# First head's operands copied within SBUF, and the last node of a two-branch attention block made with features on partitions and direct products

## The reference

```python
x  = attn_x                          # (2, 1024, 128)
xn = layernorm(x)
out = x + attn(xn) + ffn(xn)

def attn(x):     # 16 heads of 8, causal, rotary embedding on q and k
    q, k, v = split_heads(x @ qkv_w.T + qkv_b)
    p = softmax(where(causal, rope(q) @ rope(k).T / sqrt(8), min))
    return merge_heads(p @ v) @ out_w.T + out_b

def ffn(inputs): # 6 nodes; each an unmasked attention with 8 heads of 16
    nodes = {-1: inputs}
    for c in range(6):
        q = ew[c,0] * (nodes[c-1] @ We[eq] + be[eq])
        k = ew[c,1] * (nodes[in_k] @ We[ek] + be[ek])
        v = ew[c,2] * (nodes[in_v] @ We[ev] + be[ev])
        nodes[c] = act_w[c] * mha(q, k, v, Wq[c], Wk[c], Wv[c], Wo[c]) + q
    return layernorm(nodes[5]) * ln_g + ln_b
```

## Time and profile before

| what | value |
|---|---|
| median of three timed runs | 1428.02 us (1425.81 to 1428.82) |
| profiled execution, its own time | 1432.52 us |
| its span, first to last instruction | 1430.7 us |
| mean granted clock of TensorE | 0.986 of 2.4 GHz |
| PE busy | 1388.9 us (97%) |
| DVE busy | 1256.0 us (88%) |
| ACT busy | 1137.6 us (80%) |
| POOL busy | 447.0 us (31%) |

### The profile page before, as it was taken

How to read it: one execution, slowest core, us unless ns; L and a number is a source line. 1 busy time by engine, 2 the same in 40 slices (tenths; PEclk the granted TensorE clock), 3 DMA queues, 4 the chain that set the end, 5 groups by cost and what they waited for, 6 DMA issues and landing times.

```text
span 1430.7 us, 60748 instructions
## 1 busy us (share of the span) xinstructions
PE 1388.9 (97%) x26482; PEld 931.6 (65%) x26482; DVE 1256.0 (88%) x1557; ACT 1137.6 (80%) x2127; POOL 447.0 (31%) x932
## 2 busy tenths in 40 slices
PE   6899999999999999999999999999999999999996
PEld 5467777656667566676676665766667666667662
DVE  8788999898989889899898898998989989989784
ACT  3378888688878878888788788887888878878793
POOL 5331114334322332233323332234223432330110
PEclk9899999999999999999999999999999999999997
DMA  8131112344232332333323223333233332321212
GB/s 251 36 126 50 59 51 95 118 130 140 71 122 83 122 106 69 100 105 101 107 80 125 99 76 100 106 114 107 75 100 106 97 109 78 127 97 56 64 40 64
DMA packets 115940, 138.22 MB, mean 97 GB/s; under 512 B 14954, under 2 KB 90347, under 8 KB 115547
## 3 DMA queue, kind: packets, MB, share of 16 engines
q1 hardware_dynamic: 115675, 134.33, 29.0%
HBM read 64.90 MB, written 62.26 MB: 89 GB/s over the span
## 4 chain that ended last, share of the span: by engine, by line
PE 84%; DMA 5%; SPq 4%; DVE 3%; ACT 2%; POOL 2%; issue 1%; ACTq 0%; POOLq 0%; DVEq 0%
PE s L992 51%; PE cps L1087 24%; PE misc L992 8%; DMA qs<-mrows 3%; SPq L419 1%; ACT probs L761 1%; DMA dram_raw_b<-csb 1%; DVE neg_max L942 1%; PE misc L987 1%; SPq L387 1%; SPq L456 1%; DMA ks<-dram_qk_a 0%; DMA ks<-dram_qk_b 0%; POOL parts L585 0%; POOL xtok L644 0%
## 5 line engine op out<-in xcount | busy, mean ns | idle before, releaser
L761 ACT ACTIVATE probs<-s 128x512 f32<-128x512 f32 x1792 | 1059.2, 599 | 227.7 <-PE s L992 166.0
L942 DVE TENSOR_REDUCE neg_max<-s 128x1 f32<-128x1024 f32 x768 | 936.2, 1222 | 71.2 <-PE s L992 16.4
L992 PE MATMUL s<-qs,ks 99*32 99x512 bf16 (+2 forms) x7680 | 808.4, 371 | 8.6 <-DMA qs<-mrows 6.7
L992 PE MATMUL s<-ks,qs 96*32 96x512 bf16 (+2 forms) x7680 | 606.7, 370 | 6.3 <-DMA ks<-dram_qk_a 4.1
L1087 PE MATMUL cps<-probs,vs 128*32 128x256 f32 (+1 forms) x7552 | 590.8, 368 | 0.3 <-ACT probs L761 0.3
L992 PEld LDWEIGHTS s<-qs,ks 99*32 99x32 bf16 x7680 | 235.6, 94 | 245.2 <-ACT probs L761 101.4
L1087 PEld LDWEIGHTS cps<-probs,vs 128*32 128x32 f32 x7552 | 314.4, 110 | 77.5 <-issue 17.1
L992 PEld LDWEIGHTS s<-ks,qs 96*32 96x32 bf16 x7680 | 290.4, 97 | 90.5 <-issue 24.7
L617 POOL TENSOR_TENSOR mparts<-neg_max,zeros 128x8 bf16<-128x8 f32 x128 | 25.8, 201 | 788.7 <-DVE neg_max L942 657.1
L938 DVE CUSTOM_DVE_ANT_0 s<-s,mask_q 128x1024 f32<-128x1024 f32 (+7 forms) x256 | 188.2, 786 | 27.5 <-PE s L992 17.8
L683 POOL TENSOR_TENSOR parts<-full,zeros 128x512 bf16<-128x512 f32 x48 | 61.5, 1282 | 52.8 <-DVE full L918 52.8
(11 more groups left out here) (128 smaller groups left out, 603.2 us busy)
## 6 DMA issues: line engine op xcount, KB each, us to landing
dram_qk_b<-parts SPq DMA_DIRECT2D x48, 384.0 KB, 3.3
qs<-dram_qk_b SPq DMA_DIRECT2D x96, 192.0 KB
ks<-dram_qk_b SPq DMA_DIRECT2D x96, 192.0 KB
dram_qk_b<-parts SPq DMA_DIRECT2D x48, 256.0 KB, 3.2
dram_raw_b<-csb SPq DMA_DIRECT2D x95, 128.0 KB, 4.4
dram_qk_b<-parts SPq DMA_DIRECT2D x48, 128.0 KB, 3.2
vsrc<-srcT SPq DMA_DIRECT2D x12, 512.0 KB, 3.2
ctx_b<-dram_raw_b SPq DMA_DIRECT2D x44, 128.0 KB
```

Of the source, the lines that this page charges most:

```text
L761: nc.scalar.activation(buf[:, lo:hi], s2[bank][:, 0:hi - lo], ACT.Exp, scale=scale).then_inc(exp_done, 1)
L942: last = ve.tensor_reduce(peak, scores, AX.X, ALU.max, negate=True)
L992: last = te.matmul(dst[c0:c0 + STRIP, :], lhsT[:, c0:c0 + STRIP], rhs, start=start, stop=stop, tile_position=(0, c0))
```

## The change

Ahead of the loop:
- The layer norm of the second batch (8 tiles) moves from VectorE to GpSimd, its transposes and copies into A0 (`tr` 2 and 3). GpSimd sets the rows of ones in `ks` earlier.
- The products of the sixth node (`prod` 5) and all of the edge biases (`b0` 0 to 2, 18 matmuls of one column) move into A0; the other biases get later turns. VectorE instead of GpSimd makes the low parts n = 2, 3. `row_n` is gone.
- Head 0's second chunk is no longer read back from DRAM. Twelve copies take 8 rows of a part within SBUF from `parts` to `qs[0]` and `ks[0]`; the first chunk is written and read as before, by two loads of half the width. The writes of the second chunk follow.
- GpSimd's addition of the bias row to `xtok` moves from step 0 to step 6 of A0. Head 8 is loaded ahead of the max row of step 7, and the wait for the second batch's writes moves to the end of the first AL.

At the end:
- The last node of the first batch is made like the others (`lnode`), VectorE adds its bias, and four transposes for each chunk turn it (`fin`).
- In T only five heads of the second batch are normed through DRAM, and their sums and contexts are asked for at the end of BE. For each of the last three heads TensorE multiplies `csb` directly by that head's rows of `Wo` with a column that picks the sum (`late_head`); VectorE multiplies by the reciprocal and adds up in `fin`. The rows are placed in `late_wo` (in `ctx_a`) by twelve DMAs in BE. `TAIL_AT` puts two of these products, the skip products, the context products and the transposes of the rest into T's turns; the third product comes last.

The diff, cut to its core:

```diff
+FIN_AT = {(4, 4): ("lnode", 0), (4, 6): ("lnode", 1), (5, 1): ("fin", 0), (5, 5): ("fin", 1)}
+TAIL_AT = {(0, 2): ("direct", 0), (0, 4): ("skip", 0), (0, 6): ("skip", 1), (1, 2): ("direct", 1),
+           (1, 4): ("contexts", 0), (1, 5): ("contexts", 1), (1, 6): ("turned", 0), (1, 7): ("turned", 1)}
-START_AT = {(0, 0): ("bias", 1), (0, 1): ("bias", 2), (0, 2): ("bias", 3),
-            (0, 4): ("rot", 8), (1, 2): ("rot", 9), (1, 4): ("rot", 10), (2, 2): ("rot", 11),
+START_AT = {(0, 0): ("b0", 0), (0, 1): ("b0", 1), (0, 2): ("b0", 2), (0, 3): ("tr", 2),
+            (0, 4): ("rot", 8), (1, 0): ("tr", 3), (1, 1): ("prod", 5), (1, 3): ("bias", 1), (2, 0): ("bias", 2), (2, 3): ("bias", 3), (1, 2): ("rot", 9), (1, 4): ("rot", 10), (2, 2): ("rot", 11),
...
+            def first_head(n, part):
+
+                w, op = n // 2, n % 2
+                lo, hi, step = (Q_ROWS, K_ROWS)[op][part]
+                sp.wait_ge((rope_hi, rope_mid, a_low)[part], n + 1)
+                for r in range(lo, hi, step):
+                    sp.dma_start((qs, ks)[op][0][r * DA:(r + 1) * DA, w * CH:(w + 1) * CH], parts[n][0:DA, part, :]
+                                 ).then_inc(first_in, 16)
+
+            for n in range(NCH):
                 write_a(n, [0])
                 if n:
                     write_a(n - 1, [2])
                 write_a(n, [1])
-            write_a(2 * NCH - 1, [2])
+            sp.wait_ge(dve_const, 3 * RING)
+            first_head(2, 0)
+            write_a(1, [2])
+            first_head(2, 1)
+            first_head(3, 0)
+            first_head(2, 2)
+            for n in range(NCH):
+                sp.wait_ge(a_written[n], 3 * 16)
+                sp.dma_start((qs, ks)[n][0][0:6 * DA, 0:CH], qk_dram["A"][n, :, 0:DA, 0:CH]).then_inc(qk_in[0], 16)
+            first_head(3, 1)
+            first_head(3, 2)
+            for n in (2, 3):
+                write_a(n)
...
-                    if k == UP - 1 and kind not in ("A0", "BE", "T"):
+                    if (kind, r, k) == ("AL", 0, UP - 1):
+                        for s in a_written:
+                            sp.wait_ge(s, 2 * 3 * 16)
+                    if k == UP - 1 and kind not in ("BE", "T"):
                         load_unit(kind, r, UP, b)
...
+                    if kind == "BE" and UP - N_LATE <= k:
+
+                        n = k - (UP - N_LATE)
+                        sp.wait_ge(spread_zero, 1)
+                        for g in range(4):
+                            sp.dma_start(late_wo[g * VW:g * VW + DB, n, g, 0:D], last_wo[k * DB:(k + 1) * DB, :]
+                                         ).then_inc(spread_in, 16)
+                    if kind == "BE" and k == UP - 1:
+
+                        for n in range(2):
+                            sp.wait_ge(ctx_out[n], 16 * ((UP // 2) * (ph + 1) - 1 - n))
+                        sp.wait_ge(lnode_ps, NCH)
+                        read_before("T", 0, 1, [0], "sums")
+                        read_before("T", 0, 1, [0], "contexts")
...
+            for t in range(TB, TT):
+                pl.tensor_scalar(xn[:, t * D:(t + 1) * D], xtok[:, t * D:(t + 1) * D], mv[:, 2 * t:2 * t + 1],
+                                 rstd[:, t:t + 1], ALU.subtract, ALU.mult).then_inc(xn_late, 1)
...
-                    if kind == "A0" and k == 0:
+                    if kind == "A0" and k == 6:
 
                         pool.wait_ge(bias_used, 4)
...
+            def late_head(n, t0, tiles):
+
+                for t in range(t0, t0 + tiles):
+                    at = t % 3 * WO
+                    if t % 3 == 0 or t == t0:
+                        some = min(3 - t % 3, t0 + tiles - t)
+                        after(ve.reciprocal(rec_h[:, t:t + some],
+                                            late[t // 3][:, at + D:at + D + (some - 1) * WO + 1:WO]))
+                    dst = fin[:, S + t * D:S + (t + 1) * D]
+                    if n == 0:
+                        last = ve.tensor_scalar(dst, late[t // 3][:, at:at + D], rec_h[:, t:t + 1], None, ALU.mult)
+                    else:
+                        last = ve.scalar_tensor_tensor(dst, late[t // 3][:, at:at + D], rec_h[:, t:t + 1], dst,
+                                                       ALU.mult, ALU.add)
+                return last
...
             for n in range(1, len(FINISH)):
+                after(late_head(N_LATE - 1, FINISH[n][0] - TB, FINISH[n][1]))
                 last_moments(n)
...
+                elif what == "lnode":
+                    pe.wait_ge(ctx_ready, NORMS.after(kind, r))
+                    mm_strips(misc[:, :], last_wo, ctx_b[:, cols], stop=False)
+                    mm_strips(misc[:, :], last_we, srcT[:, (NODES - 1) * T + w * CH:(NODES - 1) * T + (w + 1) * CH],
+                              start=False).then_inc(lnode_ps, 1)
                 else:
-                    pe.wait_ge(ctx_ready, NORMS.after(kind, r))
-                    last_node(0, w, misc, ("skip", "context"))
+                    pe.wait_ge(lnode_sb, w + 1)
+                    turned(misc, full[w]).then_inc(fin_ps, 1)
...
+            def late_head(n):
+
+                pe.wait_ge(ctx_sb, UP * PHASES.before("T", 0) - N_LATE + n + 1)
+                pe.wait_ge(spread_in, 16 * 4 * N_LATE)
+                pe.wait_ge(spread_zero, 1 + N_LATE)
+                pe.wait_ge(max_done, MAXIMA.before("T", 0))
+                need(pe, dir_used, n)
+                for t in range(TB):
+                    at = t % 3 * WO
+                    last = mm(late[t // 3][:, at:at + WO], csb[(UP - N_LATE + n) % 2][:, t % 2 * 128:(t % 2 + 1) * 128],
+                              late_wo[:, n, t // 2, :])
+                last.then_inc(dir_ps, 1)
```

More of the change, by code:

```diff
@@ L439, in normed @@
                 which, heads, width = ("A", HA, DA) if kind == "B0" else ("B", HB, DB)
-                return which, heads, heads - (kind == "T"), width
+                return which, heads, heads - N_LATE * (kind == "T"), width
             def read_before(kind, r, b, which_of, what):
@@ L786, in _ @@
             walk(phase)
-            for w in range(NCH):
-                act.wait_ge(fin_ps, NCH + w + 1)
-                nc.scalar.copy(fin[:, S + w * CH:S + (w + 1) * CH], (misc, s2[0])[w][:, :]).then_inc(fin_sb, 1)
         @block.vector
@@ L944, in phase @@
-                        if NORMS.per[kind] and (k, i) == ((2, 7) if kind in ("BL", "BE", "T") else (SPREAD_AT[kind], 0)):
+                        if i == 0:
+                            need(dve, max_parts, 4 * (u - 1))
+                        n = steps_before(kind, k, 0) + i
+                        dve.wait_ge(s1_ready, MAXIMA.before(kind, r) + n + 1)
+                        for t, lo, hi in query_tiles(kind[0], i):
+                            scores, peak = s1[n % 2][:, lo:hi], neg_max[k % 2][:, t:t + 1]
+                            if kind[0] == "A":
+                                last = ve.tensor_tensor_reduce(
+                                    out=scores, in0=scores, in1=mask_q[:, S - hi + lo:S], scale=-1.0,
+                                    scalar=-MASKED, op0=ALU.add, op1=ALU.min, accum_out=peak)
+                            else:
+                                last = ve.tensor_reduce(peak, scores, AX.X, ALU.max, negate=True)
@@ L996, in _, with transposes @@
             pe.wait_ge(pool_const, 4)
-            def transposes(batch):
-                for t in range(batch * TB, (batch + 1) * TB):
-                    pe.wait_ge(xn_ready, t + 1)
-                    last = te.transpose(half[t // 4][:, t % 4 * 128:(t % 4 + 1) * 128], xn[:, t * D:(t + 1) * D],
-                                        ident[:, :])
-                    if t % 4 == 3:
-                        last.then_inc(xt_ps, 1)
+            def transposes(g, bank):
+                for t in range(4 * g, 4 * g + 4):
+                    if t < TB:
+                        pe.wait_ge(xn_ready, t + 1)
+                    else:
+                        pe.wait_ge(xn_late, t - TB + 1)
+                    last = te.transpose(bank[:, t % 4 * 128:(t % 4 + 1) * 128], xn[:, t * D:(t + 1) * D], ident[:, :])
+                last.then_inc(xt_ps, 1)
             def rotate(m, bank):
@@ L1067, in _ @@
             pe.wait_ge(rot_done, 4 * NCH)
-            biases(0)
-            for n in range(2, NODES):
-                products(n)
-            pe.wait_ge(comp_sb, 3 * NODES)
+            pe.wait_ge(comp_sb, 3 * 2)
+            pe.wait_ge(va_sb, TB // 4)
             pe.wait_ge(pool_const, N_CONST)
@@ L1142, in extra @@
                     biases(w)
+                elif what == "b0":
+                    edge_biases(w)
+                elif what == "tr":
+                    transposes(w, misc)
+                elif what == "prod":
+                    products(w)
                 elif what == "rot":
@@ new lines, in tail @@
+            def tail(what, w):
+                cols = slice(w * CH, (w + 1) * CH)
+                src = (NODES - 1) * T + S + w * CH
```

(24 more changed lines are left out.)

248 lines of the change are left out of this document (132 added, 116 removed).

## The result

The kernel after takes 1433.77 us (median of five runs, 1432.7 to 1436.13), the kernel before 1428.02 (1425.81 to 1430.58) beside it: ratio 1.0043, 95% interval 1.003 to 1.0057. It is slower by 6.1 us (4.3 to 8.1); 1426.5 was forecast, and the time lies 2.3 us above the range of 1419.5 to 1431.5. The profiled execution took 1436.13 us with a span of 1434.3.

What follows compares the result with a forecast made beforehand. TensorE, 84% of the last-ending chain, was taken as the main bound, with SP's issues at the start; +2.95 -3.3 -3.0 +7.3 -5.5 = -1.55 us took 1428.0 to 1426.5, range 1419.5 to 1431.5.

Steps and rivals of the forecast that it cites:

- Item 2: Phase A0: work moved between the first scores lengthens the first three head steps from 27.95 to 34.4 us, +6.45 us.
- rival B: Steps 0 to 2: shared-bank hand-overs cost 0.7 us each, clock falls again in step 1; 1433 us, chance 0.15.
- Item 1: Start: earlier ropes and copies inside SBUF bring the first score from 38.8 to 35.3, -3.5 us.
- Item 3: Ninth head: loading head 8 before the max row removes TensorE's gap and the clock's fall, -3.3 us.
- Item 4: Last node, first batch: products with features on partitions are cheaper, less the added transposes, -3.0 us.
- Items 5 and 6: T: inserted products and transposes are exposed, +7.3 us; after the last context 16.7 us against 22.2, -5.5 us.
- rival D: T: gathering TensorE's idle shares hides the inserted lumps by half, +3.6 instead of +7.3; 1423 us, chance 0.08.
- A: Step 0: TensorE keeps or soon regains full clock; -7.2 us with cheap issues, about 1421; chance 0.27 including issues alone.
- E: T: transposes let the clock fall, the last two direct products cost 1.4 us more each; 1429 us, chance 0.05.

Runs made afterwards that it cites:

- start_only: Start of the kernel after, with head 8's request and the tail of the kernel before: ratio 1.0046 to the kernel before, +6.6 us.
- path_only: Kernel before with head 0's second chunk copied inside SBUF, its first loaded apart, no work moved past the first score: ratio 0.9962, -5.4 us.
- after_gap: Kernel after with the edge biases and the sixth node's products issued ahead of the first score: ratio 0.9992 to the kernel before, 7.3 us below after.
- tail_only: Kernel after with the start and head 8's loads of the kernel before, only the new tail kept: ratio 0.9994 to before, -0.9 us.
- after_no_direct: Kernel after with 7 of 8 products left out of two direct groups, output incomplete: ratio 1.0016 to before, 3.9 us below after.
- after_sliced: Kernel after with the last phase's direct, skip and context products and transposes issued in slices of a few instructions: ratio 1.0042 to before.
- path_b0: path_only plus edge biases between the first scores, other biases later, POOL's input addition in step 6: ratio 1.004 to before, 5.7 us above it.
- after_filler: Kernel after with six unused 512-column matmuls in the idle stretch before the first score: ratio 1.0033 to before, 1.4 us below after.
- before_again: The unchanged kernel before, run once more for a second trace: ratio 1.0007 to the kernel before.
- gap_filler: after_gap with five unused 512-column matmuls behind the edge biases: ratio 1.0004 to the kernel before, 1.7 us above after_gap.

## Why the prediction was wrong, by its own steps

*Item 2 is the step that failed:* "what is moved into phase A0" was given +6.45 us and measured 11.7 in the trace of after (39.7 us from the first score to head 3's maxima, against 27.95) and 11.3 by start_only less path_only. A group was taken at 2.3 us and is 2.72, 1.3 us for three, and with it step 0 came to 15.7 and not 14.2 (its own terms add to 14.35 already). Step 1 was taken "at full clock again" with 9.7; the clock was at 1.2 GHz until 55.1 and again from 62.0, and the step took 12.0 (13.3 in start_only). Step 2 was 10.9, not 9.8, and the first maxima came 1.1 us behind the first score, not 0.7: 1.5+2.3+1.1+0.4 makes the 5.3 us that were missing. That is the second fall of rival B, with hand-overs of 0.2 to 0.4 us, as I had priced them. B's sum, 1433, was only 0.8 short, but by luck: 4 of its 7 us were hand-overs of 0.7 us, which did not come.

The trace of before had more to say on the clock than I read from it:

```profile
29.00:30.00 1.00, 1.00 (x8) 1.00 (x8) 1.00 (x3) 1.00 (x5) 0.73 (x1) 0.63 0.96 334
...
53.00:54.00 1.00, 1.00 (x6) 0.13 (x8) 1.00 (x5) 0.00 (x0) 0.00 (x0) 0.57 0.03 6
```

At 29.2 it falls with TensorE busy at 1.00, inside the same 36 edge-bias instructions, then ahead of the first score (from 26.36), and at 53.2 it falls a second time, in step 1, until 56.6. The second trace of before has the first of these falls (28.3) and not the second. So step 1 "at full clock" was not what the one trace at hand showed. (The falls and the rise that the prediction puts at 39.7, 107.9 and 49.6 are at 39.5, 107.7 and 49.7.)

What the runs show in place of the +6.45: at the low clock the three groups between the scores cost 6.4 us of step 0, and ahead of the first score, in the wait, they cost nothing (after_gap); the whole moved work costs 11.3 (start_only less path_only).

*Item 1 failed too.* The ropes were to come 1 to 2 us sooner without eight norms. They started at 15.56 against 15.57, since the rotations on TensorE set them, not VectorE. The first in-SBUF issue came at 25.6 and not 23.3. Issue was right (0.63 us taken, 0.62 to 0.78 seen, in the median 0.63). From the last issue to the first score it was 1.9 us (35.3 to 37.19) where I took 3.0 from the earlier trace rows. The Trainium skill, "DMA: Bandwidth & Descriptors", Anatomy of one DMA, gives about 2.0 us of fixed cost for a DMA on GpSimd's path. These went through SP, and the 1.9 measured are near it. In all -1.6 instead of -3.5. The gain was also credited in part to the freed engines: the copies alone give it whole (37.24 in path_only).

*Item 3:* -3.3 forecast, -3.5 in the trace. The step holds against both traces of before, but 2.1 of it is a fall of the clock that four changed kernels with the late load did not have; alone the edit measured -2.0 (interval -3.9 to -0.1), and on top of the copies nothing that can be told.

*Item 4:* -3.0 forecast, -2.5 seen: the step with the products is 4.1 us shorter, the step with the transposes 1.6 longer and not 1.0.

*Items 5 and 6:* +7.3 and -5.5 forecast, +7.5 and -5.8 seen. tail_only bears out the sum of 4 to 6 (-0.9 against -1.2), after_no_direct that the lumps are exposed, and after_sliced that rival D was no way out: TensorE has no time to gather in T.

*Rivals.* A is false: the clock was low already before the first score. (Its sum was off too: -1.55-5.7 is the clock alone, without the cheap issues that it names.) E has nothing for it: the direct products at 1393.67, 1407.16 and 1418.38 took 2.05 each, and the granted clock is 1.00 from 1405 to 1421, with the transposes at 1415.01 and 1416.58 in it. That POOL's late addition on the input stays hidden in step 6 was seen (103.87, 4.61 us, in a step of 6.95 us against 6.87).

*Open.* Whether the clock falls at the ninth head because the gap is 1.8 us long and not 1.3 to 1.5 stays open; before's share of runs with it is not known either. Why the clock falls while TensorE works through one-column groups, and what a full clock through step 0 would give, is open too. So is a part of the copies' gain: the medians give 4.6 to 5.4 us, the rows of the trace place 2.8 to 4.3. How the moved work splits is known to about 2 us only, as trace and median of path_b0 differ by that. On the hand-overs through the one bank there is only the reading of the trace; no run took them out.

## What to carry to other kernels

Before work is moved out of the lead to the first result, find which engine or queue that result waits for: here it was SP's chain of issues and TensorE's rotations, so that freeing VectorE and TensorE bought little or nothing (in two of the traces with the moved work the first score came 1.2 us sooner), and 11 us were paid for work that had stood in the wait's shadow. Measure a change of many parts in parts: one of them (twelve small copies) was worth -5 us and was buried under another of +11. And where a forecast gain is partly a fall of the clock, take a second trace of the same kernel and one of a neighbour first: the gap was there every time with the late load, the fall's 2.1 us was not.

## What the runs showed of the hardware that I had not expected

- The granted clock fell while the records showed TensorE busy at 1.00: in after_filler from 1.00 to 0.50 at 41.5, with no gap, behind two groups of twelve one-column f32 matmuls with bf16 scores between; in before at 29.2 and in before_again at 28.3, 2.8 and 2.3 us into 36 such matmul instructions in a row. In gap_filler the same 36 (29.79 to 33.87) ran through at 1.00, and the fall came at 34.6. A group of twelve takes 1.50 us at the full clock and 2.72 at the low one.
- An idle gap of TensorE at the ninth head was followed by a fall where it was 1.81 and 1.82 us long (two traces of before) and by none where it was 1.30 to 1.54 (four traces).
- An f32 product of one tile takes 0.25 us in a run of its like (1.99 for eight) and lengthens a turn of bf16 scores by 0.39 (after_sliced).
- A copy of 8 rows within SBUF takes SP 0.63 us to issue, and the first score that waits for the last one starts 1.9 us after that issue begins, where copies of 16 rows landed after 3.0.
